# Graph attention on one core: the small VectorE ops of the row factor lose their second SBUF operand, and GpSimd folds twice instead of three times

## The reference

```python
# x: (32, 256, 512), adj: (32, 256, 256), four weights of (512, 512), 16 heads of 32
h = relu(layernorm(x))
q, k, v = split_heads(h @ Wq.T), split_heads(h @ Wk.T), split_heads(h @ Wv.T)
a = einsum('bhnd,bhmd->bhnm', q, k) * 512 ** -0.5 + (adj + adj)
row_nonzero = any(a != 0, axis=-1)          # a row of only zeros gives an output of zero
p = softmax(where(row_nonzero, a, -inf)); p = where(isnan(p), 0, p)
o = einsum('bhnm,bhmd->bhnd', p, v)         # heads joined again
x = x + o @ Wo.T
```

## Time and profile before

| | |
|---|---|
| median of 3 runs | 1376.79 us (1375.9 to 1376.99) |
| profiled execution, its span from first to last instruction | 1374.0 us |
| PE busy | 1302.3 us, 95% |
| DVE busy | 1260.6 us, 92% |
| ACT busy | 1041.4 us, 76% |
| POOL busy | 1015.0 us, 74% |
| mean granted clock of PE | 0.993 of full speed |

### The profile page before, as it was taken

One profiled execution on the slowest core, in us unless ns is written; L12 is line 12 of the kernel. 1 busy time (PEld: TensorE's weight loads), 2 busy tenths in 40 slices (PEclk: granted clock), 3 DMA queues, 4 the chain that ended last, 5 costly groups with the idle time before them and its releaser, 6 DMA issues. The chain is left out here.

```text
span 1374.0 us, 44286 instructions
## 1 busy us (share of the span) xinstructions
PE 1302.3 (95%) x13072; PEld 1230.5 (90%) x13072; DVE 1260.6 (92%) x4279; ACT 1041.4 (76%) x2379; POOL 1015.0 (74%) x1519
## 2 busy tenths in 40 slices
PE   5999999999999999999999999999999999999996
PEld 4889999999999999999999999999999999999985
DVE  6999999999999999999999999999999999999995
ACT  3777778777778777787777787777787777787784
POOL 5777777777778777777777777777777777777775
PEclk9999999999999999999999999999999999999997
DMA  6435444445344445354454454354454454444441
GB/s 214 110 92 139 107 121 122 118 119 136 100 130 115 115 129 123 104 140 115 106 138 115 107 142 112 105 145 106 116 127 117 115 137 104 125 116 120 108 119 43
DMA packets 90772, 163.88 MB, mean 119 GB/s; under 512 B 14976, under 2 KB 23168, under 8 KB 90752
## 3 DMA queue, kind: packets, MB, share of 16 engines
q1 hardware_dynamic: 90752, 163.64, 46.0%
HBM read 46.14 MB, written 16.78 MB: 46 GB/s over the span
## 5 line engine op out<-in xcount | busy, mean ns | idle before, releaser
L855 POOL TENSOR_TENSOR fold<-minus 128x512 f32<-128x512 f32 x256 | 329.0, 1285 | 249.3 <-DVE minus_max L698 249.3
L549 ACT ACTIVATE probs<-minus,minus_max 128x256 f32<-128x256 f32 x1024 | 461.5, 500 | 58.2 <-DVE minus_max L698 58.0
L559 ACT ACTIVATE pT_hi<-pT_ps 128x512 f16<-128x512 f32 x512 | 306.1, 598 | 150.9 <-PE pT_ps L397 149.1
L698 DVE CUSTOM_DVE_ANT_0 minus<-s_ps,adj_now 128x256 f32<-128x256 f32 x1024 | 388.7, 415 | 21.9 <-PE s_ps L386 16.2
L716 DVE TENSOR_TENSOR pT_lo<-pT_ps,pT_hi 128x512 f16<-128x512 f32 x512 | 348.4, 680 | 58.0 <-ACT pT_hi L559 57.8
L397 PE MATMUL pT_ps<-ident,probs 128*128 128x128 f32 x2048 | 308.9, 273 | 1.3 <-ACT probs L549 1.3
L324 PE MATMUL job_ps<-hT_hi,w_hi 128*128 128x256 f32 x1024 | 299.4, 292 | 3.4 <-DVE hT_lo L666 2.9
L324 PE MATMUL job_ps<-hT_lo,w_hi 128*128 128x256 f32 x1024 | 289.2, 282 | 0.0
L324 PE MATMUL job_ps<-hT_hi,w_lo 128*128 128x256 f32 x1024 | 288.7, 282 | 0.0
L397 PEld LDWEIGHTS pT_ps<-ident,probs 128*128 128x128 f32 x2048 | 241.3, 141 | 15.1 <-ACT probs L549 2.4
L386 PE MATMUL s_ps<-qk_stack 96*128 96x256 f32 x1024 | 247.7, 324 | 2.1 <-DMA qk_stack<-qk_parts 2.0
(11 more groups left out here) (82 smaller groups left out, 2651.0 us busy)
## 6 DMA issues: line engine op xcount, KB each, us to landing
qk_stack<-qk_parts SPq DMA_DIRECT2D x768, 128.0 KB, 2.3
x_in<-x SPq DMA_DIRECT2D x32, 512.0 KB, 3.4
x_res<-x SPq DMA_DIRECT2D x32, 512.0 KB, 3.6
out<-y SPq DMA_DIRECT2D x64, 256.0 KB, 2.1
adj_in<-adj SPq DMA_DIRECT2D x32, 256.0 KB, 3.5
minus<-wq_t SPq DMA_DIRECT2D x2, 512.0 KB, 5.0
qk_parts<-wv SPq DMA_DIRECT2D x2, 512.0 KB, 8.7
y<-wk_t SPq DMA_DIRECT2D x1, 512.0 KB, 6.7
```

The costliest lines, as they stand in the source:

```text
L549: end = nc.scalar.activation(probs[hh % 2][:, t, :], minus[hh // 2 % 2][:, hh % 2, t, :], ACT.Exp, bias=minus_max[:, hh // 2 % 4, hh % 2, ...
L559: nc.scalar.activation(pT_hi[hh % 4][:, :, :], pT_ps[hh % 2][:, :].rearrange("p (m n) -> p m n", m=NT), ACT.Copy).then_inc(pT_high, 1)
L698: end = nc.vector.tensor_tensor_reduce(out=minus[pair % 2][:, hh % 2, t, :], in0=s_ps[SCORE_BANK[hh]][:, t * N:(t + 1) * N], in1=adj_now[: ...
L855: nc.gpsimd.tensor_tensor(f1[:, :, :], src[:, :, 0:N // 2], src[:, :, N // 2:N], ALU.add).then_inc(folded1, 1)
```

## The change

The third fold on GpSimd is dropped. The second one writes its 64 values a row into a new tile `bounds`, whose 65th column is the row's minimum, written there by `shift`. DVE's reduction then takes all 65 values a row and gives the greatest absolute value, so it answers in one instruction what L725 and L734 did in two. The reciprocal reads the row sums from `o_ps` in PSUM and not from `o_raw` in SBUF, and writes its result to column 96 of each stretch of `o_ps`, which no matmul writes. The last small op reads `some` in SBUF and that column in PSUM, and moves from behind `low_probs` to ahead of it. `values` of an even head waits for `factor_ready` instead of `o_copied`, since DVE now reads `o_ps` until then.

```diff
@@ attention_block @@
+    FREE = 3 * HD
...
-        minus_max = sb("minus_max", [P, 4, 2, NT])
+        BOUND = N // 4
+        bounds = sb("bounds", [P, 4, 2 * NT, BOUND + 1])
         fold1 = [sb(f"fold1_{i}", [P, 2 * NT, N // 2]) for i in range(2)]
-        fold2 = [sb(f"fold2_{i}", [P, 2 * NT, N // 4]) for i in range(2)]
-        fold3 = [sb(f"fold3_{i}", [P, 2 * NT, N // 8]) for i in range(2)]
-        some = [sb(f"some{i}", [P, 4, 2 * NT]) for i in range(2)]
+        some = [sb(f"some{i}", [P, 2 * NT]) for i in range(2)]
+        factor = [sb(f"factor{i}", [P, 2 * NT]) for i in range(2)]
...
         o_ps = psum("o_ps")
+        o_sums = o_ps[:, :].rearrange("p (q c) -> p q c", c=P)
@@ TensorE: values @@
                 if hh % 2 == 0 and not early:
-                    pe.wait_ge(o_copied, b * PAIRS + hh // 2)
+                    pe.wait_ge(factor_ready, b * PAIRS + hh // 2)
@@ ScalarE: exponentials @@
                     end = nc.scalar.activation(probs[hh % 2][:, t, :], minus[hh // 2 % 2][:, hh % 2, t, :], ACT.Exp,
-                                               bias=minus_max[:, hh // 2 % 4, hh % 2, t:t + 1], scale=-1.0)
+                                               bias=bounds[:, hh // 2 % 4, 2 * (hh % 2) + t, BOUND:BOUND + 1],
+                                               scale=-1.0)
@@ VectorE: shift @@
-                        accum_out=minus_max[:, pair % 4, hh % 2, t:t + 1])
+                        accum_out=bounds[:, pair % 4, 2 * (hh % 2) + t, BOUND:BOUND + 1])
@@ VectorE: the small ops @@
-            def factor1(b, pair):
-                dve.wait_ge(folded3, b * PAIRS + (pair + 1))
-                nc.vector.tensor_reduce(some[pair % 2][:, 0, :], fold3[pair % 2][:, :, :], AX_X,
-                                        ALU.add).then_inc(some_ready, 1)
+            def any_nonzero(b, pair):
+                dve.wait_ge(folded2, b * PAIRS + (pair + 1))
+                nc.vector.tensor_reduce(some[pair % 2][:, :], bounds[:, pair % 4, :, :], AX_X, ALU.max,
+                                        apply_absolute_value=True).then_inc(some_ready, 1)
                 dve.wait_ge(o_copied, b * PAIRS + (pair + 1))
-                nc.vector.reciprocal(some[pair % 2][:, 1, :], o_raw[pair % 2][:, :, ONES]).then_inc(rcp_ready, 1)
+                nc.vector.reciprocal(o_sums[:, :, FREE], o_sums[:, :, ONES]).then_inc(rcp_ready, 1)
-            def factor2(b, pair):
+            def factors(b, pair, early):
                 dve.wait_ge(some_ready, b * PAIRS + (pair + 1))
-                nc.vector.scalar_tensor_tensor(some[pair % 2][:, 2, :],
-                                               minus_max[:, pair % 4, :, :].rearrange("p h t -> p (h t)"), 0.0,
-                                               some[pair % 2][:, 0, :], ALU.not_equal, ALU.max).then_inc(keep_ready, 1)
-            def factor3(b, pair, early):
                 dve.wait_ge(rcp_ready, b * PAIRS + (pair + 1))
-                dve.wait_ge(keep_ready, b * PAIRS + (pair + 1))
                 if not early:
                     dve.wait_ge(o_ready, b * PAIRS + (pair - 1))
-                nc.vector.scalar_tensor_tensor(some[pair % 2][:, 3, :], some[pair % 2][:, 2, :], 0.0,
-                                               some[pair % 2][:, 1, :], ALU.not_equal,
-                                               ALU.mult).then_inc(factor_ready, 1)
+                nc.vector.scalar_tensor_tensor(factor[pair % 2][:, :], some[pair % 2][:, :], 0.0,
+                                               o_sums[:, :, FREE], ALU.not_equal, ALU.mult).then_inc(factor_ready, 1)
@@ VectorE: body @@
-                        factor1(*pair)
+                        any_nonzero(*pair)
                     for kind, n, d in ended_before(hh, first, last):
                         take(kind, n, b + d)
                     if pair:
-                        factor2(*pair)
+                        factors(*pair, first and hh < 6)
                     low_probs(b, hh, first and hh < 2)
-                    if pair:
-                        factor3(*pair, first and hh < 6)
@@ GpSimd: divide, fold @@
-                    some[pair % 2][:, 3, :].rearrange("p (h t) -> p h t", h=2).unsqueeze(3).to_broadcast([P, 2, NT, HD]),
+                    factor[pair % 2][:, :].rearrange("p (h t) -> p h t", h=2).unsqueeze(3).to_broadcast([P, 2, NT, HD]),
...
-                f1, f2, f3 = fold1[pair % 2], fold2[pair % 2], fold3[pair % 2]
+                f1, f2 = fold1[pair % 2], bounds[:, pair % 4, :, 0:BOUND]
...
                 pool.wait_ge(folded1, b * PAIRS + (pair + 1))
-                nc.gpsimd.tensor_tensor(f2[:, :, :], f1[:, :, 0:N // 4], f1[:, :, N // 4:N // 2],
-                                        ALU.add).then_inc(folded2, 1)
-                pool.wait_ge(folded2, b * PAIRS + (pair + 1))
                 if not early:
                     pool.wait_ge(some_ready, b * PAIRS + (pair - 1))
-                nc.gpsimd.tensor_tensor(f3[:, :, :], f2[:, :, 0:N // 8], f2[:, :, N // 8:N // 4],
-                                        ALU.add).then_inc(folded3, 1)
+                nc.gpsimd.tensor_tensor(f2, f1[:, :, 0:N // 4], f1[:, :, N // 4:N // 2],
+                                        ALU.add).then_inc(folded2, 1)
```

More of the change, by code:

```diff
@@ L191, in attention_block @@
         pv_done, folded1 = sem("pv_done"), sem("folded1")
-        folded2, folded3 = sem("folded2"), sem("folded3")
-        some_ready, keep_ready = sem("some_ready"), sem("keep_ready")
-        rcp_ready, factor_ready, o_ready = sem("rcp_ready"), sem("factor_ready"), sem("o_ready")
+        folded2 = sem("folded2")
+        some_ready, rcp_ready = sem("some_ready"), sem("rcp_ready")
+        factor_ready, o_ready = sem("factor_ready"), sem("o_ready")
         o_added = sem("o_added")
@@ L792, in _ @@
             body(B - 1, False, True)
-            factor1(B - 1, PAIRS - 1)
-            factor2(B - 1, PAIRS - 1)
-            factor3(B - 1, PAIRS - 1, False)
+            any_nonzero(B - 1, PAIRS - 1)
+            factors(B - 1, PAIRS - 1, False)
             take("o", 1, B - 1)
```

## The result

The changed kernel takes 1318.8 us (median of 4 runs, 1315.97 to 1319.87) against 1376.89 before: a ratio of 0.957 (95% interval 0.956 to 0.959), 4.3% faster. The forecast was 1332 with a range of 1325 to 1350. So the direction and the place were right, but the forecast gain was too small: 58 us came where I expected 45. The profiled execution spans 1318.1 us, 55.9 less than the 1374.0 before.

The account below looks back on a forecast made before the run. PE was taken as the bound, stalled 1.43 us a batch by a late DVE. Terms of -41.5, -3.5, -1.5 and +1.5 took the span from 1374.0 to 1329.0; with 2.8 for the runs' median, 1332 us, range 1325 to 1350.

Parts of the forecast that it names:

- L734 is held by the fold: In DVE's slots 15 and 1, L734, with two SBUF operands, lasts until GpSimd's first fold ends; median 1134 ns.
- the small ops stay blocked: Rival: the factors in slot 1 still end with the fold; 0.1 to 0.3 us a batch slower, 1380 to 1386; chance 0.06.
- Reduction +0.14: DVE's reduction reads 65 instead of 32 values a row: 0.14 us longer, 256 times, +35 us of DVE.
- The reciprocal in PSUM: DVE's reciprocal reading and writing PSUM costs nothing extra; bounds nothing and one more op of 0.17 us.
- Waiting for its result: The last small op on DVE starts 0.20 us after the reciprocal instead of 0.12: +0.08.
- the walk: Start times through DVE's slots 15, 0 and 1: L716 in slot 1 at 660.87 instead of 662.42, ending at 661.55.
- The remaining stall: What is left of PE's 1.43 us stall in slot 2: 0.05 in 30 batches, +1.5 us in the sum.
- the 0.12 that I had to spare: In slot 2 PE could go on at 661.61 and was due at 661.73, so the stall is just gone.
- The other terms: Outside regular batches: -3.5 us for other `pT_lo` waits, -1.5 for `hT_lo` in the first and `oT_lo` in the last batch.
- The third fold and PE's new wait at nothing: Dropping GpSimd's third fold alone is worth nothing; PE waiting for `factor_ready` instead of `o_copied` costs nothing.
- What is late next: The transposes of `h`, due at 667.05, need `h` and `v`; both are in time by 0.3 to 0.4 us.
- more than the stall goes: Rival: below 1325 us, if every small delay of first and last batch vanishes too; chance 0.05.

Follow-up runs that it names:

- experiment 3: The changed kernel with only the reciprocal back in SBUF, so the last small op has two SBUF operands again: 1349.4 us, ratio 0.980.
- experiment 5: The kernel before, nothing removed, but GpSimd's first fold of a pair waits until the L734 beside it is done: 1354.2 us, ratio 0.984.
- experiment 2: The changed kernel, but GpSimd folds three times and the reduction takes 33 values a row: 1320.1 us, ratio 0.960.
- experiment 9: The changed kernel with the last small op behind `low_probs` again, its operands as changed: 1316.7 us, ratio 0.956.
- experiment 7: Layer norm's moments computed a batch earlier, in slot 6: 1429.7 us from the kernel before, 1346.8 us from the changed one.

## Why the prediction was right and wrong

- *What bounds the kernel.* Right that PE sets the pace and loses time to a late DVE in slot 2. The sentence that failed is "In the regular batches it is the only long gap between PE's products. So a batch is about 40.10 us of PE and one stall of 1.43 us". The word "long" hid two stalls of 0.12 and 0.14 us. PE's bare batch was at most 39.83 us, and 29 x 0.26 = 7.5 of the missing us lie there.
- *The missing 13.0 us in full* (1331.8 less 1318.8). In the regular batches 49.3 us came and I had 40.0: 9.3, which are the 7.5 just named, 0.9 for the remaining stall and 0.9 in small steps. Outside them 6.6 came and I had 5.0: 1.6. The last 2.1 are neither: the runs' median lay 2.8 us above the profiled span before and 0.7 after, and I carried the 2.8 over.
- *L734 is held by the fold.* Right: experiment 3 brings it back with one operand, experiment 5 takes it away with one wait. The rival that the small ops stay blocked fell.
- *The terms.* Reduction +0.14: right (419 against 277 ns). The reciprocal in PSUM: 15 ns more, near the end of my range that I took. Waiting for its result: 0.37 from its start and not 0.20, the term of the walk that was mis-sized. Of the 0.17, experiment 3 shows 0.07 with the result in SBUF (638.43 to 638.70), and the other 0.10 comes with PSUM. The walk also said that `low_probs` of slot 0 is not held; it waits 0.17 us for ACT's `pT_hi`.
- *The remaining stall*, +1.5 us in the sum for 0.05 a batch: 0.02 was left. Two errors went against me: the walk was 0.33 us too short, and PE was due 0.12 earlier than I took, because the small stall ahead of it went too. One went the other way: measured against PE, DVE came to slot 15 0.33 us earlier than I let it. With the 0.12 that I had to spare they cancel. That the long stall is just gone, as forecast, is in part luck.
- *The other terms.* For all that is not a regular batch I took 5.0 us; it was 6.6. In the last batch the shifts of a pair lie 3.26 us apart instead of 4.15 (from 1286.14 to 1289.40).
- *The third fold and PE's new wait at nothing.* Right as far as can be measured: 0.06 us a batch for the fold and the longer reduction (experiment 2), and 0.08 us for the place with its wait (39.83 against the 39.75 of experiment 9).
- *What is late next.* `h` has 0.38 us of room in slot 4 with two folds (it ends at 602.64, its transposes start at 603.02) and none with three; the margin was real and didn't bind.
- *DVE's busy time*: I said about 1070 us, it is 1130. I took off whole durations, but neighbours on DVE overlap, and 39 us of overlap went with the ops; the copy of `adj` grew by 0.5 us a batch, 15 us.
- *The range.* Its low end came from first and last batch alone. I gave "more than the stall goes" 0.05 and looked for it in the wrong place: a late engine is late at every meeting, not only at the one that the waits list.

## What to carry to other kernels

A wait list shows only stalls longer than a matmul is drawn. Before taking "period minus the visible stall" as an engine's own time, compare the distances between starts with the shortest ones of the same kind, at every point where that engine meets the late one. If a tiny op of one engine ends when another engine's long op ends, see whether they share a way to SBUF, and change one operand; and treat all such ops together, since the next one takes the freed meeting.

## What the runs showed of the hardware

- A small DVE op with two SBUF operands that meets a running GpSimd fold ends 0.02 to 0.03 us behind the fold: all 162 such instances of L734 in the kernel before and all 224 in experiment 3 (there 638.70 + 0.87 against 638.26 + 1.29). With one operand in PSUM no one of 256 was over 159 ns, though 224 of them stand beside a running fold. The Trainium skill (SBUF — State Buffer, Who interferes with whom) states this lock for two SBUF inputs against a GpSimd instruction that reads SBUF; these traces agree.
- Not every meeting holds. In the kernel before, an L734 starts at 666.45, 0.06 us behind the start of `normalise` (L823, 666.39), and lasts 0.15 us; so do the 29 others in that place. In experiment 3 the small op starts 0.54 us behind `normalise` and ends with it. No run tests why.
- The copy of `adj`, one source in SBUF and no second operand, is held too: 0.91 us in 30 of 32 instances of the changed kernel, where it starts 0.11 us behind the start of GpSimd's second fold and ends 0.28 behind its end. Before, it started 0.06 us ahead of the fold's end and took 0.41. What this costs no run isolates: the next shift starts 0.47 us behind the copy's end in both traces, and in slot 0 DVE then waits 0.17 us for ACT.
- Reading and writing PSUM made the reciprocal 15 ns longer (181 against 166), and the next op, which needs the result, starts 0.20 us after its end instead of 0.10 in experiment 3. By the Trainium skill's fixed parts (VectorE: DVE Perf Modes, the TRN2 errata), 120 cycles with a PSUM source against 58 at 0.96 GHz, it would have been 65 ns longer, an estimate; the measurement does not agree.
- Behind a stall of 2.00 us PE worked for 3 us at a granted clock of 0.50 (experiment 7).
